# AdaLN block on one core: the uses of the spare PSUM bank move behind the next unit's scores

## The reference

```python
mod = (silu(c) @ wmod).reshape(2, 6, 1, -1)          # sa, ca, ga, sb, cb, gb; |ga|, |gb| at least 0.25
h = layernorm(x) * (1 + ca) + sa
x = x + ga * attention(h)                            # 16 heads of 8 features, q = k = v = h
h = layernorm(x) * (1 + cb) + sb
x = x + gb * ffn(h)
# attention: softmax(q q^T / sqrt(8) * m) q, with m = 1 where the two token numbers agree mod 8, sigmoid(ipw) elsewhere
# ffn: relu(h sW1 + sb1) sW2 + sb2, plus the 3 most probable of 15 experts (softmax router),
#      each relu(h eW1 + eb1) eW2 + eb2, weighted by its probability
```

## Time and profile before

| what | before |
|---|---|
| median of 3 runs | 373.64 us (372.37 to 373.94) |
| the profiled execution's own time | 373.84 us |
| its span | 372.1 us |
| PE busy | 338.4 us, 91% |
| ACT busy | 288.0 us, 77% |
| DVE busy | 185.9 us, 50% |
| POOL busy | 33.0 us, 9% |
| first and last exponential start | 23.9 and 262.5 us |

### The profile page before, as it was taken

One profiled execution on the slowest core, in us unless ns is written; L12 is line 12 of the kernel. 1 busy time (PEld: TensorE's weight loads), 2 busy tenths in 40 slices (PEclk: granted clock), 3 DMA queues, 4 the chain that ended last, 5 costly groups with the idle time before them and its releaser, 6 DMA issues.

```text
span 372.1 us, 6245 instructions
## 1 busy us (share of the span) xinstructions
PE 338.4 (91%) x2365; PEld 153.6 (41%) x2365; DVE 185.9 (50%) x499; ACT 288.0 (77%) x265; POOL 33.0 (9%) x47
## 2 busy tenths in 40 slices
PE   3849899999999998999989899999989999999995
PEld 2532322222323322333222333223458577777773
DVE  6993113533442310425513525101489988797884
ACT  3647999999999999999999999999525344444442
POOL 4891000521000000100000100000010000000000
PEclk9999999999999999999999999999999999999998
DMA  7785899024000399200000000930200089460000
GB/s 218 252 304 175 290 348 295 4 82 174 2 0 5 131 322 384 99 2 3 2 2 0 2 0 7 409 128 2 113 1 2 0 318 405 157 202 26 28 2 29
DMA packets 23631, 45.78 MB, mean 123 GB/s; under 512 B 2254, under 2 KB 10096, under 8 KB 22060
## 3 DMA queue, kind: packets, MB, share of 16 engines
q1 hardware_dynamic: 23160, 44.92, 34.2%
q10 hardware_dynamic: 436, 0.39, 0.3%
HBM read 31.56 MB, written 13.75 MB: 122 GB/s over the span
## 4 chain that ended last, share of the span: by engine, by line
PE 61%; DVE 13%; issue 11%; ACT 10%; DMA 2%; POOL 1%; ACTq 0%; DVEq 0%
PE acc L1302 23%; PE slot L1190 13%; ACT prob L661 10%; PE spare L1142 4%; PE slot L1332 3%; PE slot L1334 3%; PE slot L1333 3%; PE slot L1357 3%; DVE oT L970 3%; PE slot L1355 2%; PE slot L1354 2%; PE slot L1349 2%; DVE prob L1098 2%; DVE glo L1106 2%; DMA wcol<-attn_inter_palace_weight 2%
## 5 line engine op out<-in xcount | busy, mean ns | idle before, releaser
L661 ACT ACTIVATE prob<-slot 128x1536 f32<-128x1536 f32 x171 | 234.7, 1469 | 11.2 <-PE slot L1190 10.7
L1302 PE MATMUL acc<-prob,val 128*9 128x512 f32 x1024 | 135.1, 600 | 5.2 <-DVE oT L970 4.7
L1190 PE MATMUL slot<-QQ,KK 32*128 32x512 f32 (+1 forms) x768 | 92.9, 409 | 10.5 <-issue 5.1
L1190 PEld LDWEIGHTS slot<-QQ,KK 32*128 32x128 f32 x768 | 43.9, 187 | 129.4 <-ACT prob L661 87.2
L690 ACT ACTIVATE ghi<-prob 128x512 fp32r<-128x512 f32 x52 | 32.9, 632 | 50.6 <-DVE prob L1098 49.9
L970 DVE COPY oT<-acc 128x512 f32<-128x512 f32 x16 | 11.1, 691 | 84.5 <-PE acc L1302 84.5
L1106 DVE SCALAR_TENSOR_TENSOR glo<-prob,ghi 128x512 fp32r<-128x512 f32 x52 | 35.5, 682 | 0.4
L1098 DVE SCALAR_TENSOR_TENSOR prob<-slot,bcol,KK 128x512 f32<-128x512 f32 x37 | 27.6, 749 | 6.8 <-PE slot L1334 6.5
L1332 PE MATMUL slot<-h2hi,w1h 128*128 128x512 f32 x64 | 30.6, 478 | 0.0
L1302 PEld LDWEIGHTS acc<-prob,val 128*9 128x9 f32 x1024 | 15.5, 88 | 34.2 <-issue 29.2
L547 POOL TENSOR_TENSOR rstd<-rstd,power 128x4 f32<-128x4 f32 (+1 forms) x6 | 7.4, 1229 | 233.7 <-DVE rstd L764 233.7
(11 more groups left out here) (179 smaller groups left out, 247.7 us busy)
## 6 DMA issues: line engine op xcount, KB each, us to landing
KK<-cw_d SPq DMA_DIRECT2D x7, 1024.0 KB, 8.5
rows<-cw_d SPq DMA_DIRECT2D x5, 1024.0 KB, 5.1
KK<-kd SPq DMA_DIRECT2D x14, 256.0 KB, 5.2
QQ<-qd SPq DMA_DIRECT2D x14, 256.0 KB, 5.5
KK<-kw SPq DMA_DIRECT2D x14, 256.0 KB, 6.4
KK<-cw_d SPq DMA_DIRECT2D x3, 768.0 KB, 9.0
rows<-in_L_ffn_eW SPq DMA_DIRECT2D x2, 960.0 KB, 7.4
kd<-w2h SPq DMA_DIRECT2D x2, 512.0 KB, 5.3
```

The source lines that it names most:

```text
L661: nc.scalar.activation(ring[:, at:at + n * CH], slot[u % 2][:, 0:n * CH], ACT.Exp, scale=SCALE).then_inc(exp_done, 1)
L1190: return mm(dst, KK[n][r, s, c * M:(c + 1) * M], QQ[n][r, lo:hi], start=True, stop=True, tile_position=(32 * q, 0))
L1302: last = mm(acc[32 * q:32 * q + HD + 1], val[:, b, n, c, q, :], prob[:, (G * cl + q) % RING], start=c == 0, stop=c == C - 1, tile_position ...
```

## The change

The unit at which a class is weighed is counted one higher (`last_unit(cl) + 3`), and on PE the weighing of a unit stands ahead of its scores instead of behind. The units of all uses of the spare bank, of DVE's norms and of the choice of experts are one higher too.

```diff
 def weigh_unit(cl):
-    return last_unit(cl) + 2
+    return last_unit(cl) + 3
...
-TURNS = ((0, 1, 2), (1, 0, 38), (1, 1, 70))
-BIAS_UNIT = 18
-SECOND_UNIT = 27
-ROUTE = ((47, 50, 54, 59, 62), (91, 94, 98, 103, 106), (131, 134, 138, 143, 146))
+TURNS = ((0, 1, 3), (1, 0, 39), (1, 1, 71))
+BIAS_UNIT = 19
+SECOND_UNIT = 28
+ROUTE = ((48, 51, 55, 60, 63), (92, 95, 99, 104, 107), (132, 135, 139, 144, 147))
...
-        free = (u for u in range(end_unit(sec) + 1, UNITS) if u % 4 == 2 and u not in taken_units)
+        free = (u for u in range(end_unit(sec) + 1, UNITS) if u % 4 == 3 and u not in taken_units)
...
-                scores(u)
                 for cl in WEIGH.get(u, []):
                     weigh(cl)
+                scores(u)
                 for use in SIDE.get(u, []):
                     side(use)
-            for u in range(UNITS, UNITS + 3):
+            for u in range(UNITS, UNITS + 4):
```

## The result

The changed kernel takes **376.75 us** (median of 11 runs) against 373.84 for the one before (11 runs, same chip): ratio 1.0066, 95% interval 1.0046 to 1.0086. By the medians it is slower by 2.9 us (forecast 377.0, +3.2); the interval of the ratio is 1.7 to 3.2 us. The profiled execution has a span of 375.3 us against 372.1. In the runs further down, one execution (379.35 us, three logits alone) was in a slower state of the chip and is left out of its median and ratio.

The account below looks back on a forecast made before the run. ACT was taken to pace attention at 1.33 us per unit, losing 12.5 us to late scores. The moved uses summed to +3.3 us, giving 377.0 us (376.0 to 378.2 for this case alone), range 374.2 to 379.4.

Parts of the forecast that it names:

- What paces attention: Attention's exponentials: ACT takes one unit per 1.33 us and loses 12.5 us to late scores; PE has slack per cycle.
- 0.4 to 0.6 us in front of scores at each use: Sign expected in the next profile: PE idle this long in front of scores at each use, where before was none.
- The walk: Durations carried through all 171 units in both orders: ACT's loss 12.1 us before, 15.4 after.
- The two edits cancel: Weighing one unit later but in front of scores leaves the order of scores and weighings on PE: cost nothing.
- The moved uses cost PE's slack: 28 spare-bank uses now stand behind scores, ahead of three units slower than ACT; slack is spent idle: sum +3.3 us.
- The tally by kinds: Split of the sum: start +0.47, turns +0.98, two zT +0.35, logits +0.88, cwT +0.76, bias 0, h2T -0.04, between sites -0.08.
- DVE's cover for the first zT: At unit 3, DVE takes zT at 32.18 whatever PE does, behind its own 4.51 us; rows and loads keep their times.
- The start (+0.47): First zT at unit 3: scores of 3 start earlier, exponential 4 comes at 31.47 against 30.93; a little comes back.
- The rival of the slow start: A new 0.54 us pause on PE delays its clock's rise by one unit: +1.2, 378.2 us; chance 0.08.
- The rival of ACT's lead: With a little more PE slack, ACT's lead hides the moved uses; only the start is lost: 374.3 us; chance 0.14.
- The rival "faster": Scores no longer wait behind uses awaiting DVE: about 0.6 us back at seven sites, 370.1 us; chance 0.06.
- Dearer sites: Each of 28 uses costs the slack it no longer fills, 0.42 us: 385.6 us, half that 379.7; chance 0.08.

Follow-up runs that it names:

- three logits alone: Kernel before, with only the three logit uses moved behind the next unit's scores: 374.38 us against 373.82, ratio 1.0018.
- the uses back in front: Changed kernel, with each use of the spare bank issued ahead of its unit's scores again: 374.47 us against 373.65 for the kernel before.
- the run with four: Kernel before, with only the three h2T and the turn of section 5 moved behind the next unit's scores: 372.37 us against 373.82, ratio 0.9960.
- the run with h2T alone: Kernel before, with only the three h2T moved behind the next unit's scores: 372.91 us against 373.65, ratio 0.9975.
- the run with eleven: Kernel before, with eleven uses placed where a computed schedule of all units found room: 372.77 us against 373.82, ratio 0.9956.

## Why the prediction was right

- **What paces attention** (ACT at 1.33 us, PE's slack in front of the scores with u % 4 = 3). Right: stretch +2.9, the rest unchanged, PE's waits in front of scores up from 4.8 to 7.3 us. The sign "0.4 to 0.6 us in front of scores at each use" came at few: the places above 0.15 us rose from 11 to 18, and of the 28 uses only five have 0.36 us or more in front of their scores (zT at 27.07 is one). The walk itself had 0.18 us at the turn of section 1; the slack of a whole cycle rarely meets in front of one instruction.
- **The two edits cancel.** Right: -0.03 us with the uses back in front, with everything else of the change in place.
- **The moved uses cost PE's slack.** Right in kind and in sum: +3.3 booked, +3.2 in span, +2.9 in the stretch of exponentials, +2.9 in the medians. On the part without the start the walk was 0.66 too high (2.77 against 2.11), and before exponential 30 it was too low: some 0.5 of its 3.3 lie there, 0.8 us in the profiles. That the two partly cancel in the total is luck. Why the walk is too high isn't known; for the turns alone it is 0.5 too low.
- **The tally by kinds** is the step that failed. It booked turns +0.98, logits +0.88 and h2T -0.04, as what happened between neighbouring sites, and +1.11 for cwT and two zT. Alone, turns cost 3.26, logits 0.51, and h2T gain 1.38; that adds up to 2.39 where the change has 2.11, so that for cwT and zT nothing is left. In the change the gain of h2T and the cost of the turns ahead of them meet in the same cycle: the turn of the same stage, issued later, takes away the time in which DVE gets h2f ready. The sum held because the walk had both in it; its parts can't be moved one by one.
- **DVE's cover for the first zT** was misread. The 4.51 us in the earlier trace rows are idle time in front of DVE's instruction, ended by nothing that the profile shows, and not work of DVE's. Nor did the taker keep its time of 32.18: it starts at 33.64 after the change, but at 33.71 with the uses back in front too, so the change isn't shown to be the cause, and PE waits for no load in either.

```profile
33.64 0.81 DVE L877 TENSOR_SCALAR bH<-spare,caf,modF 128x512 f32<-128x512 f32 x1 [5.66 <-issue]
```

- **The start (+0.47).** A delay of 0.4 to 0.5 us at exponential 4 was measured in three runs (7.51, 7.47, 7.37 after the first, against 7.00). It isn't shown that any of it lasts to exponential 6, and the remaining 0.2 us of the change's start can't be laid to it, since the kernel with the old order had +1.0 in one run. So 0.7 of the profiled 2.9 us may be the moment at which PE became fast in that execution.
- **The rival of the slow start** had the pause as its cause. Nothing of that is seen: with a pause of 0.44 us PE was fast at 30.81 in one run, without it still slow at 33.91 in another. One execution of each can't exclude a small part.
- **The rival of ACT's lead** (374.3, +0.5) falls: the lower end of the ratio is +1.7 us.
- **The rival "faster"** fell for the change as a whole, but its mechanism is real: uses that wait for DVE gain behind scores, about 0.45 us at each h2T and 0.2 at the turn of section 5, where the rival had 0.6. It needs those uses alone; the run with four is 0.4% faster than the kernel before. Dearer sites (0.42 at each) are refuted by 2.11 us for 24 uses.

## What to carry to other kernels

When two engines nearly match, look for the one instruction in front of which the slower-paced cycle leaves slack, and put short side work there, ahead of the wait and not behind it. Side work whose input isn't ready does the opposite: it turns the slack of the engine into a stall for the work behind it, so let the next independent piece go first. Carry durations through the whole order before trusting a sum of single moves, and take the engines that deliver the inputs into it: where DVE and the loads were left out, a promised 3.8 us became 1.1 to 1.8.

## What the runs showed of the hardware

**When PE becomes fast varies by microseconds between executions.** Weighings of the same shape take 1.90 us, then 1.04. In the kernel before, the rate rises during the weighing that starts at 30.81 (1.57); in the run with the uses back in front, with the same order on PE, during the one at 33.91 (1.37); in the run with h2T alone the scores at 25.80 are fast already (0.56 instead of 0.90). The granted clock reads 1.00 there all the while the earlier trace rows, although the matmuls are slow. Where PE had been fast before, the column does show it: behind the wait of 2.85 us in the run with h2T alone, the weighing at 46.82 takes the same 1.90 us at a granted clock of 0.50, the level of 1.2 GHz. The third number from the end is the granted clock:

```profile
46.80:48.70 1.90, 1.90 (x14) 0.18 (x11) 0.00 (x0) 1.45 (x1) 0.00 (x0) 0.50 0.93 312
```

Behind the wait of 1.20 us for a load in the run with eleven, the matmuls stayed fast (scores 0.50, weighing 1.05). With zT in its old place, exponential 6 comes 10.02 to 11.38 us after the first, a spread of 1.4 us. The Trainium skill (TensorE: Matmul & The Clock Gate, Part 1: The HAM clock gate) says that the warm-up varies from run to run for the same kernel. These profiles, of kernels whose order on PE is the same up to there, agree; the spread that the page gives, 500 ns either way, is less than the 2 to 3 us between the rises of these two.

**The time before attention varies too**, and part of it is given back. The first exponential started between 19.76 and 24.38 us in the profiled executions. At 19.76 the scores of unit 16 then waited 2.85 us for their loads, which they don't in the kernel before; with the logits alone (first exponential at 22.48) PE waited 1.18 us for loads at unit 21, of section 2. So the loads of the first sections are just in time.
